# A four-stage sequence kernel: signs flipped earlier in the recurrence's GpSimd order, TensorE's moving reads stored side by side, and the third stage's first loads put ahead of its constants

## What is computed

```
x = x + ssm(layernorm(x))                    # scan over 4096 steps, state 64 per channel, out_proj
x = x + layernorm(x) @ expert_w[0].T + expert_b[0]
# L1 attention, on xn = layernorm(layernorm(x)) * ln_scale + ln_bias
w = sigmoid(xn @ Wx.T @ Ww.T + bw); k = xn @ Wk.T; v = xn @ Wv.T; r = sigmoid(xn @ Wr.T)
state = (1 - w_t)[:, None] * state + k_t[:, None] * v_t[None, :];  out_t = r_t @ state;  y = out @ Wo.T
# L1 feed-forward: signs of the normed row times cluster signs pick one of 64 tiles of 8 columns,
# whose columns go through a spline
```

## Time and profile before

| | us |
|---|---|
| median of 3 runs | 7978.18 (7977.69 to 7981.29) |
| the profiled execution's own time | 7975.57 |
| its span in the trace | 7973.8 |
| start of the third stage (first DMA issue) | 5133.16 |
| start of the fourth stage (first DMA issue) | 6653.34 |
| start of the fifth stage (first idle on the chain that ended last) | 7736 |

### The profile page before, as it was taken

How to read it: one execution, slowest core, us unless ns; L and a number is a source line. 1 busy time by engine, 2 the same in 40 slices (tenths; PEclk the granted TensorE clock), 3 DMA queues, 4 the chain that set the end, 5 groups by cost and what they waited for, 6 DMA issues and landing times. The chain is left out here.

```text
span 7973.8 us, 217784 instructions
## 1 busy us (share of the span) xinstructions
PE 7210.3 (90%) x74510; PEld 5270.5 (66%) x74510; DVE 6579.7 (83%) x8089; ACT 4783.8 (60%) x10953; POOL 5927.6 (74%) x3528
## 2 busy tenths in 40 slices
PE   8799999999999999999999999889999997999964
PEld 4577777777777777777777777644444444666642
DVE  7799999999999999999999999723223235999976
ACT  7778877878888877878778878511111112444430
POOL 1499999999999999999999999700000003999964
PEclk9999999999999999999999999999999998999975
DMA  6500000000000000000000000112222122333324
GB/s 211 160 0 17 17 0 17 17 0 17 17 0 17 17 0 17 17 0 17 17 0 17 17 0 6 66 53 90 83 86 74 74 80 94 101 100 97 100 89 158
DMA packets 198187, 389.94 MB, mean 49 GB/s; under 512 B 26224, under 2 KB 51888, under 8 KB 186544
## 3 DMA queue, kind: packets, MB, share of 16 engines
q1 hardware_dynamic: 189088, 370.45, 14.0%
q10 hardware_dynamic: 8976, 17.83, 0.6%
HBM read 208.52 MB, written 179.70 MB: 49 GB/s over the span
## 5 line engine op out<-in xcount | busy, mean ns | idle before, releaser
L494 POOL TENSOR_TENSOR scan_hc<-scan_h,scan_cb 128x1024 f32<-128x1024 f32 x2048 | 4776.4, 2367 | 103.4 <-PE scan_y L617 82.2
L659 DVE TENSOR_TENSOR_SCAN scan_h<-scan_a,scan_carry,scan_u 128x512 f32<-128x512 f32 x4096 | 4800.2, 1255 | 16.3 <-PE scan_u L606 8.5
L606 PE MATMUL scan_u<-scan_dg,scan_v 64*128 64x128 f32 x32768 | 2379.8, 285 | 314.0 <-DVE scan_h L659 269.4
L553 ACT ACTIVATE scan_a<-scan_dt,scan_aneg 128x512 f32<-128x512 f32 x4096 | 2658.4, 708 | 7.4 <-ACT scan_yo L533 7.4
L606 PEld LDWEIGHTS scan_u<-scan_dg,scan_v 64*128 64x128 f32 x32768 | 1990.5, 187 | 793.9 <-DVE scan_h L659 556.1
L617 PE MATMUL scan_y<-scan_ident,scan_hc 128*128 128x128 f32 x16408 | 2250.8, 280 | 14.3 <-ACT scan_yo L533 9.9
L617 PEld LDWEIGHTS scan_y<-scan_ident,scan_hc 128*128 128x128 f32 x16408 | 1757.4, 140 | 272.9 <-ACT scan_yo L533 15.7
L524 ACT ACTIVATE scan_dg<-scan_half,scan_bt 128x64 f32<-128x64 f32 x4096 | 1138.8, 341 | 5.8 <-DVE scan_onward L645 5.1
L164 POOL TENSOR_TENSOR mid_r<-mid_ve,mid_half_neg 128x4 f32<-128x4 f32 x32 | 32.4, 1012 | 1284.5 <-DVE mid_ve L132 795.6
L545 ACT ACTIVATE scan_carry<-scan_h,scan_onward 128x4 f32 (+1 forms) x1008 | 302.9, 300 | 934.8 <-DVE scan_h L659 934.7
L865 ACT ACTIVATE mid_rt<-mid_pb 128x512 f32<-128x512 f32 x64 | 38.2, 598 | 610.1 <-PE mid_pb L929 610.1
(11 more groups left out here) (214 smaller groups left out, 6902.1 us busy)
## 6 DMA issues: line engine op xcount, KB each, us to landing
scratch_y<-scan_yo ACTq DMA_DIRECT2D x17, 1024.0 KB, 4.3
pre_x<-in_x SPq DMA_DIRECT2D x16, 1024.0 KB, 5.7
scratch_dt<-pre_dt SPq DMA_DIRECT2D x16, 1024.0 KB, 5.8
scratch_vr<-pre_vr SPq DMA_DIRECT2D x16, 1024.0 KB, 4.7
scan_dt<-scratch_dt SPq DMA_DIRECT2D x16, 1024.0 KB, 5.3
scan_v<-scratch_vr SPq DMA_DIRECT2D x32, 512.0 KB, 7.6
mid_yr<-scratch_y SPq DMA_DIRECT2D x16, 1024.0 KB, 7.0
mid_x<-in_x SPq DMA_DIRECT2D x16, 1024.0 KB, 8.1
```

The source lines that it names most:

```text
L494: pool.tensor_tensor(hc[:, q].rearrange("p n (r j) -> p n r j", j=P), h[:, q].rearrange("p n (r j) -> p n r j", j=P), cb[:, bass.ds(b * NS ...
L553: ins = act.activation(a[:, q, n, :], dt[:, par, q, :], ACT.Exp, scale=aneg[:, q, bass.ds(m * 2 + n, 1)])
L606: mm = pe.matmul(u_ps[:, q % 2, g, k * HP:(k + 1) * HP, :], v[row, par, k, q, :], dg[row, buf, k], start=True, stop=True)
L659: ins = dve.tensor_tensor_scan(h[:, q, n, :], a[:, q, n, :], u_ps[:, q % 2, :, :, n].rearrange("p g t -> p (g t)"), carry[:, q, bass.ds(m ...
```

## The change

1. Third stage, SyncE: `load` of chunk 0 (y, scale, x) is issued first, then all constants in a new order with four semaphores: skip, ident, wout (`rows_consts`), w0, b0, ns, nb, bw (`ffn_consts`), wx, ww (`fold_in`), wk, wr, wv (`proj_consts`), then `load` of chunk 1. VectorE waits at its start for `rows_consts` (48: its three DMAs) in place of all 11.
2. Third stage, TensorE and ScalarE: the product `wxw` is no longer made first. Half of it is made behind chunk 0's `attn_out` and half behind its `ffn`, in `pb` in place of `pa`, and ScalarE copies it in four pieces behind its copies of `ht`.
3. Fourth stage, GpSimd: `ends_keys` is split into `ends_keys` (`kl`) and `ends_reads` (`ql`), and the order of those pieces becomes `ends_keys(+3), flip(+1), ends_reads(+3), totals(+3)`. `flip` waits for step 2 of `act_r` in place of all 6.
4. Fourth stage, ScalarE: `signs` comes ahead of `kept`.
5. Fourth stage: `qr` and `ql` get the layout of `kc` and `kl` (sub-steps innermost). GpSimd writes them through `steps()`, TensorE reads them without.

```
...
-consts = sem("consts"); ticks_dve = sem("ticks_dve"); half_ready = sem("half_ready"); bwn_ready = sem("bwn_ready")
+rows_consts = sem("rows_consts"); ffn_consts = sem("ffn_consts"); proj_consts = sem("proj_consts"); ticks_dve = sem("ticks_dve"); half_ready = sem("half_ready"); bwn_ready = sem("bwn_ready")
...
-CONSTS = 11
...
 @block.sync
 def _(sp):
-    for dst, src in ((w["wx"], wx_d), (w["ww"], ww_d)):
-        sp.dma_start(dst[:], src).then_inc(fold_in, 16)
-    loads = [(w["wout"], wout_d), (w["w0"], w0_d), (w["wk"], wk_d), (w["wr"], wr_d), (w["wv"], wv_d),
-             (b0, b0_d.partition_broadcast(P)), (skip, skip_d.partition_broadcast(P)), (ident, ident_d), (ns, ns_d), (nb, nb_d), (bw, bw_d)]
-    for dst, src in loads:
-        sp.dma_start(dst[:], src).then_inc(consts, 16)
+
+    def consts():
+        for dst, src in ((skip, skip_d.partition_broadcast(P)), (ident, ident_d), (w["wout"], wout_d)):
+            sp.dma_start(dst[:], src).then_inc(rows_consts, 16)
+        for dst, src in ((w["w0"], w0_d), (b0, b0_d.partition_broadcast(P)), (ns, ns_d), (nb, nb_d), (bw, bw_d)):
+            sp.dma_start(dst[:], src).then_inc(ffn_consts, 16)
+        for dst, src in ((w["wx"], wx_d), (w["ww"], ww_d)):
+            sp.dma_start(dst[:], src).then_inc(fold_in, 16)
+        for dst, src in ((w["wk"], wk_d), (w["wr"], wr_d), (w["wv"], wv_d)):
+            sp.dma_start(dst[:], src).then_inc(proj_consts, 16)
...
 def load(c, par, half):
+        if isinstance(c, int) and c == 0:
+            consts()
     def store_x2(c, par, half):
...
-    pool.wait_ge(consts, CONSTS * 16)
+    pool.wait_ge(ffn_consts, 80)
     def roots(c, par, half):
...
-    dve.wait_ge(consts, CONSTS * 16)
+    dve.wait_ge(rows_consts, 48)
 @block.scalar
 def _(act):
-    act.wait_ge(consts, CONSTS * 16)
-    act.mul(bwn[:], bw[:], -1.0).then_inc(bwn_ready, 1)
-    act.wait_ge(bwn_ready, 1)
-
-    act.wait_ge(folded, 1)
-    act.copy(wxw[:], pa[:]).then_inc(wxw_ready, 1)
     def turned_y(c, par, half):
 def turned_h(c, par, half):
+        if isinstance(c, int) and c == 0:
+            act.wait_ge(ffn_consts, 80)
+            act.mul(bwn[:], bw[:], -1.0).then_inc(bwn_ready, 1)
+            act.wait_ge(bwn_ready, 1)
+            for q in range(Q):
+                act.wait_ge(folded, q + 1)
+                act.copy(wxw[:, q], pb[:, q]).then_inc(wxw_ready, 1)
     def decays(c, par, half):
...
 def _(pe):
-    pe.wait_ge(fold_in, 32)
-
-    for q in range(Q):
-        for i in range(Q):
-            mm = pe.matmul(pa[:, q, :], w["wx"][:, i, q * P:(q + 1) * P], w["ww"][:, i, :], start=(i == 0), stop=(i == Q - 1))
-    mm.then_inc(folded, 1)
-    pe.wait_ge(wxw_ready, 1)
-    pe.wait_ge(consts, CONSTS * 16)
+
+    def fold(rows):
+
+        pe.wait_ge(fold_in, 32)
+        for q in rows:
+            for i in range(Q):
+                mm = pe.matmul(pb[:, q, :], w["wx"][:, i, q * P:(q + 1) * P], w["ww"][:, i, :], start=(i == 0), stop=(i == Q - 1))
+            mm.then_inc(folded, 1)
     def turn_y(c, par, half):
+        if isinstance(c, int) and c == 0:
+            pe.wait_ge(rows_consts, 48)
 def attn_out(c, par, half):
+        if isinstance(c, int) and c == 0:
+            fold(range(Q // 2))
     def turn(src):
...
     def ffn(c, par, half):
+        if isinstance(c, int) and c == 0:
+            pe.wait_ge(ffn_consts, 80)
+        if isinstance(c, int) and c == 0:
+            fold(range(Q // 2, Q))
+            pe.wait_ge(wxw_ready, Q)
+            pe.wait_ge(proj_consts, 48)
     def turn_xn(c, par, half):
...
-kc = sb("kc", [P, 2, LEVELS - 1, C // 2, SUB]); qr = sb("qr", [P, 2, LEVELS - 1, SUB, C // 2])
-kl = sb("kl", [P, 2, C, SUB]); ql = sb("ql", [P, 2, SUB, C])
+kc = sb("kc", [P, 2, LEVELS - 1, C // 2, SUB]); qr = sb("qr", [P, 2, LEVELS - 1, C // 2, SUB])
+kl = sb("kl", [P, 2, C, SUB]); ql = sb("ql", [P, 2, C, SUB])
...
-R_XN, R_KEPT = 1, 5
+R_XN, R_SIGNS, R_KEPT = 1, 2, 6
 def by_tile(row):
...
-        src, dst, e = (rk[:, par, SUB], steps(kc[:, par, l - 1]), 0) if kind else (first[:, par, 0:SUB], qr[:, par, l - 1], 1)
+        src, dst, e = (rk[:, par, SUB], steps(kc[:, par, l - 1]), 0) if kind else (first[:, par, 0:SUB], steps(qr[:, par, l - 1]), 1)
     def keys(i, par, m):
...
     def ends_keys(i, par, m):
-        for kind, src, dst in ((1, rk[:, par, SUB], steps(kl[:, par])), (0, first[:, par, 0:SUB], ql[:, par])):
-            f = far[LEVELS][:, kind * C:(kind + 1) * C].rearrange("p (o c) -> p o c", o=1).broadcast_to([P, SUB, C])
-            pool_a.inc(pool.tensor_tensor(dst, src, f, ALU.mult))
+        to_end(1, rk[:, par, SUB], steps(kl[:, par]))
+
+    def to_end(kind, src, dst):
+        f = far[LEVELS][:, kind * C:(kind + 1) * C].rearrange("p (o c) -> p o c", o=1).broadcast_to([P, SUB, C])
+        pool_a.inc(pool.tensor_tensor(dst, src, f, ALU.mult))
+
+    def ends_reads(i, par, m):
+        to_end(0, first[:, par, 0:SUB], steps(ql[:, par]))
     def totals(i, par, m):
...
     def flip(i, par, m):
-        act_r.wait_all(pool, i)
+        act_r.wait(pool, i, R_SIGNS)
     def pick(i, par, m):
...
-    pipelined(pool, ITEMS, [(3, more_keys), (1, root), (3, last_keys), (1, features), (3, ends_keys), (3, totals), (1, flip), (4, keys), (1, pick)])
+    pipelined(pool, ITEMS, [(3, more_keys), (1, root), (3, last_keys), (1, features), (3, ends_keys), (1, flip), (3, ends_reads), (3, totals), (4, keys), (1, pick)])
 @block.vector
 def _(dve):
...
     def outputs(i, par, m):
-    pipelined(act, ITEMS, [(4, own_reads), (3, pad_keys), (1, normed), (2, attended), (3, scores), (1, kept), (1, signs), (2, outputs)])
+    pipelined(act, ITEMS, [(4, own_reads), (3, pad_keys), (1, normed), (2, attended), (3, scores), (1, signs), (1, kept), (2, outputs)])
 @block.tensor
 def _(pe):
...
-                            reads = steps(qr[hr, par, l - 1, :, b:b + size])
+                            reads = qr[hr, par, l - 1, b:b + size].rearrange("p n j -> p (n j)")
...
-            pe.matmul(o_ps[:, q, :], s[:, par, q, :], steps(ql[:, par, :, q * NI:(q + 1) * NI]), start=(q == 0), stop=True, skip_group_check=True)
+            pe.matmul(o_ps[:, q, :], s[:, par, q, :], ql[:, par, q * NI:(q + 1) * NI].rearrange("p i j -> p (i j)"), start=(q == 0), stop=True, skip_group_check=True)
```

## The result

The changed kernel takes 7955.1 us, the median of 8 runs (7947.97 to 7957.97); the kernel before, timed on the same chip, 7978.85 (7975.54 to 7981.29). The ratio is 0.9969, 95% interval 0.9958 to 0.998: 23.8 us gained, 16 to 34 by the interval. 7955 had been predicted. The profiled execution took 7956.88 us with a span of 7955.1.

The account below looks back on a forecast made before the run. Bounds: a chain behind late loads, with TensorE gaps, starts the third stage; VectorE held by GpSimd's products limits the fourth's loop. 22.7 - 0.7 + 1.0 = 23.0 us gained gave 7955, range 7935 to 7963 (8 in 10).

Parts of the forecast that it names:

- Loads: Third stage's start: issuing chunk 0's y, scale and x first lets `skips` start earlier, gaining 15.8 us (15.0 to 17.5).
- The fold's place: Third stage, TensorE: the weights' product fills two 7.85 us gaps and keeps the clock up; net gain 6.9 us.
- The second rival: Third stage: clock behaves otherwise and small-row loads share queues; only 13 to 16 us gained, 7962 to 7965; chance 0.13.
- The flip: Fourth stage's loop: VectorE's 0.22 us wait goes but gains zero, as L1349 is held until GpSimd's product ends.
- the naive 17 us: Fourth stage's loop: 56 turns times 0.3 us, from L1345 starting earlier once the wait for the flip is gone.
- The first rival: Fourth stage's loop: flip's gain is real, `kc` coming later or the hold being otherwise; 17 us more, 7938; chance 0.18.
- Layouts: Fourth stage: faster reads worth nothing in the loop, strided writes lose 0.7 us, last turns gain 1 us (0 to 3).
- Slower by the clock: Fourth stage's loop: TensorE's longer idle time keeps it at 1.2 GHz through its products; 162 us lost, 8117; chance 0.04.
- The sum: Third and fourth stages together: 22.7 - 0.7 + 1.0 = 23.0 us gained.

Follow-up runs that it names:

- the experiment: The changed kernel with the third stage's constants issued ahead of chunk 0's y and x again, the fold staying in TensorE's gaps: 7970.2 us.
- the spare products: The kernel with sums and key in PSUM, plus eleven third-stage products over w_out that nothing reads, placed in TensorE's waits: 7918.39 us.
- the order alone: The kernel before with only signs ahead of `kept` and flip ahead of `ql`, old layouts and third stage: 7977.57 us.
- the order without the hold: The kernel with sums and key in PSUM, but signs and flip back in the old order: 7939.58 us, 16.4 more than with the early flip.
- the sums alone in PSUM: The changed kernel with only the eight-group sums `ts` in PSUM and the key in SBUF: 7956.68 us.
- both in PSUM: The changed kernel with the eight-group sums `ts` and the key in a free part of `at_ps` in PSUM: 7923.22 us.

## Why the prediction was right, and where it was not

**Loads, right.** Forecast 15.8 us (15.0 to 17.5), measured 16.45 in the trace of the change, and 15.1 (medians) to 17 (traces) by undoing it alone. `skips` started 12.2 us behind the first issue; 12.8 had been taken. What ended last was, as supposed, wout and not x. One slip in the sum: 5133.16 + 5.7 + 2.5 is 5141.4, not 5141.0, which takes 0.4 us off the upper bound of the gain and changes nothing else.

**The fold's place, wrong.** This is the term that failed: "Net gain 6.9 us (4.0 to 7.8)". It measured 0.9 us by the time line of the experiment, and 1.0 as the stage's 17.5 less 16.45. Step by step, from the first `skips` to chunk 1's `attn_out`: the transposes of h and of xn, behind the two filled gaps, took 1.7 us less each, as forecast. `ffn` was to gain 1.8 and gained nothing, `attn_out` was to lose 0.9 and lost 1.7, `decay`'s first half was to gain 0.9 and lost 0.3. The transposes of the next y were to gain 1.7 and gave nothing, and the wait ahead of them took 0.66 of what those of xn had won: formerly released by ScalarE after 2.94 us, they now wait 3.60 for VectorE's `skips` of chunk 1, since with the fill VectorE's own chain (norm, then `skips` to 5215.48) had become the later one, a wait that the prediction didn't name.

The step of reasoning that failed is this: a busy stretch in front was taken as enough to keep the clock for all that follows. `ffn` stands behind transposes of 1.97 us and then 2.14 us of ScalarE's copies, and the clock, still granted through the wait, fell inside the product. For `attn_out` the prediction took it that the product of the weights ahead had kept it clocked. The trace of before doesn't bear that out. By 5164 the clock had fallen, the transposes of chunk 0's y (from 5167.58) took 3.65 us, and then it stood at 1.00 through the same wait of 2.14 us and into `attn_out` (from 5173.37):

```profile
5164.00:5166.00 2.00, 0.00 (x0) 0.00 (x0) 1.96 (x4) 0.00 (x0) 0.00 (x0) 0.50 0.97 357
...
5172.00:5174.00 2.00, 0.63 (x2) 0.39 (x3) 0.00 (x0) 1.31 (x3) 0.00 (x0) 1.00 0.00 0
5174.00:5176.00 2.00, 2.00 (x6) 0.85 (x5) 0.00 (x0) 0.00 (x0) 0.00 (x0) 1.00 0.04 8
5176.00:5178.00 2.00, 2.00 (x6) 0.95 (x5) 0.69 (x1) 0.00 (x0) 0.00 (x0) 1.00 0.00 0
```

So a wait of 2.14 us right ahead goes with a fall in one kernel and not in the other. The same holds for the 3.60 us ahead of the next y's transposes, which run in 3.67 us in the change and in 1.96 with the spare products. The run with spare products shows that work in and ahead of these waits prevents the falls inside `attn_out` and `ffn`; what decides in the other cases stays open. The second rival (13 to 16 us gained in all) had this mechanism in part and was nearer for this stage, at 17.5 measured against the forecast's 22.7; its other half, slower loads, didn't come.

**The flip, right, with its mechanism.** No gain of the naive 17 us: the wait of 0.22 us gone, the key's product longer by 0.34, the turn 15.84 us. Its premise held too: `kc` hangs on the end of `decays` and not on the flip (0.78 us behind it, 0.77 before). Four runs bear it out: the order alone changes nothing, the order without the hold brings 16 to 17 us, the sums alone in PSUM move the hold to the next instruction, both in PSUM remove it. The first rival's condition, that `kc` no longer leads L1349, didn't come: it leads by 0.17 us.

**Layouts, right in the loop, short outside it.** TensorE's reads fell by 0.85 us a turn and the turn didn't move. GpSimd's strided writes cost nothing (0.7 us had been put down). The first and last turns were worth about 3.4 us where 1.0 (0 to 3) had been put: it was costed by one or two reads' worth in the tail, and the 1.65 us at the start were left out.

**Slower by the clock, refuted.** The loop's granted clock is 0.94 where it was 0.93, although TensorE waits more, and `outputs` still take 3.70 us.

**The sum** of the parts was 23.0 us and measured 21.2 in the two stages: 5.9 too much for the fold's place, 0.65 too little for the loads, 3.4 too little for the fourth stage. That errors of both signs nearly cancelled, and that the medians lie 23.8 us apart where the two profiled spans lie 18.7, which is the scatter of single runs, makes the total look better foreseen than it was: the hit to a microsecond is luck.

## What to carry to other kernels

Where VectorE's small instructions run beside GpSimd, read their durations in several turns: one that varies (0.23, 0.42, 0.76 us) and always ends just behind a GpSimd instruction is held. Here no earlier start ahead of it was worth anything until both held instructions of that row read PSUM; moving them to a place beside no GpSimd product wasn't tried. For the first item of a stage, put its own loads first and count in megabytes what stands ahead of them. A filled gap on TensorE brought the clock for the transposes right behind it (0.98 and 1.08 us of wait between) and not for the product after the next wait, of 2.14 us. Don't count the clock further than that without a trace; cost each instruction from the granted clock of the windows around it.

## What was not expected of the hardware

- TensorE's clock can fall after the wait and not in it: 1.00 through the end of 16 transposes and most of a wait of 2.14 us (5184 to 5186), 0.50 two to four microseconds later, near the start of a product that had been running from 5186.43. The fall costs 1.7 us a product, and two spare products inside the wait, with one ahead of the transposes, prevented it. In the kernel before the same wait ahead of `attn_out` had no fall behind it. The Trainium skill, TensorE: Matmul & The Clock Gate, Part 1, has the clock fall after idleness; this trace adds that the fall can show inside the work that follows.
- The hold passes on: freeing one instruction lengthened the next from 0.37 to 0.87 us, to 0.06 us behind the end of GpSimd's product.
- The same 8 products of 128 columns take 2.01 us where the moving operand is read in steps of 256 bytes, and 1.16 where it lies together.
